# A gated feed-forward stage behind attention: down projection with integer weights and transposed sums

## The reference, cut to what matters

```
q = (qweight nibbles), zp = (z + 1) * s          # s: scale of (group, column), z: zero point
W = q * s[group] - zp[group]
gate = ln(x) @ Wg ;  up = ln(x) @ Wu             # 512 -> 1376
inter = gate * sigmoid(gate) * up
out = (inter @ Wd).astype(float16)               # 1376 -> 512, 11 groups of input rows
x = x + tanh(g_ffn) * out
```

## Time and profile before

| | |
|---|---|
| median of three runs | 739.44 us |
| profiled execution | 740.38 us |
| its span | 738.3 us |
| TensorE busy | 698.6 us (95%) |
| VectorE busy | 582.4 us (79%) |
| ScalarE busy | 431.5 us (58%) |
| GpSimd busy | 226.2 us (31%) |
| granted TensorE clock | 0.999 of full speed |

### The profile page before, as it was taken

How to read it: one execution, slowest core, us unless ns; L and a number is a source line. 1 busy time by engine, 2 the same in 40 slices (tenths; PEclk the granted TensorE clock), 3 DMA queues, 4 the chain that set the end, 5 groups by cost and what they waited for, 6 DMA issues and landing times.

```text
span 738.3 us, 14782 instructions
## 1 busy us (share of the span) xinstructions
PE 698.6 (95%) x5063; PEld 374.4 (51%) x5063; DVE 582.4 (79%) x779; ACT 431.5 (58%) x764; POOL 226.2 (31%) x344
## 2 busy tenths in 40 slices
PE   5879999999999999999999988999999999999997
PEld 4544555455455545554554443445455555555455
DVE  6467788887888887888877488988788778877885
ACT  4866686677677766866775645454444453334443
POOL 5312213222222222132242766583221112222221
PEclk9999999999999999999999999999999999999999
DMA  4112311331233022202202000000000000000101
GB/s 107 32 51 49 89 58 41 93 88 38 59 89 88 8 76 73 60 21 77 73 11 95 8 2 2 1 1 0 1 30 28 1 0 28 28 0 0 43 14 57
DMA packets 29196, 29.90 MB, mean 41 GB/s; under 512 B 18628, under 2 KB 18756, under 8 KB 29036
## 3 DMA queue, kind: packets, MB, share of 16 engines
q1 hardware_dynamic: 26756, 28.80, 14.2%
q10 hardware_dynamic: 2408, 0.70, 0.4%
HBM read 23.49 MB, written 4.23 MB: 38 GB/s over the span
## 4 chain that ended last, share of the span: by engine, by line
PE 66%; POOL 8%; issue 6%; ACT 6%; DMA 6%; DVE 5%; SPq 2%; ACTq 0%; POOLq 0%; DVEq 0%
PE pair L1167 13%; PE small L948 7%; PE pair L905 6%; PE small L919 5%; PE pair L1148 5%; PE pair L1149 5%; PE small L1148 4%; PE small L935 4%; PE small L1149 4%; DMA rn_rows<-rn_parts 3%; POOL rn_sq L407 3%; PE pair L884 3%; ACT eq L616 3%; PE small L985 2%; PE pair L1020 2%
## 5 line engine op out<-in xcount | busy, mean ns | idle before, releaser
L1329 DVE TENSOR_TENSOR eq<-eq,pair 128x1024 f32<-128x1024 f32 x64 | 78.1, 1220 | 52.2 <-PE pair L1002 52.2
L1415 DVE SCALAR_TENSOR_TENSOR acc<-small,scale_T,acc 128x512 f32<-128x512 f32 (+1 forms) x132 | 94.1, 750 | 30.6 <-PE small L1149 30.1
L740 ACT ACTIVATE act_gate<-acc 128x512 f32<-128x512 f32 (+1 forms) x44 | 27.8, 631 | 141.5 <-DVE acc L1415 141.5
L508 POOL TENSOR_TENSOR in_lo<-inter,in_hi 128x512 fp32r<-128x512 f32 (+1 forms) x44 | 56.5, 1283 | 175.2 <-ACT in_hi L747 175.2
L1415 DVE SCALAR_TENSOR_TENSOR acc<-pair,scale_T,acc 128x512 f32<-128x512 f32 (+1 forms) x132 | 94.4, 748 | 16.0 <-PE pair L1149 15.0
L1148 PE MATMUL pair<-ek,w_gu 128*128 (+3 forms) x220 | 85.6, 389 | 8.3 <-DVE acc L1415 6.4
L607 ACT ACTIVATE ek<-pair,kneg 128x512 f32<-128x512 f32 x128 | 86.7, 686 | 10.5 <-DVE kneg L1324 10.4
L1167 PE MATMUL pair<-wd_hi,in_hi 128*128 128x512 f32 (+1 forms) x176 | 87.0, 533 | 0.0
L1167 PE MATMUL pair<-wd_lo,in_hi 128*128 128x512 f32 (+1 forms) x176 | 86.8, 531 | 0.0
L1321 DVE TENSOR_REDUCE qmax<-pair 128x16 f32<-128x1024 f32 x64 | 77.6, 1213 | 8.1 <-PE pair L884 8.1
L1149 PE MATMUL pair<-ekT,w_gu 128*128 (+3 forms) x220 | 83.4, 379 | 0.0
(11 more groups left out here) (159 smaller groups left out, 1329.5 us busy)
## 6 DMA issues: line engine op xcount, KB each, us to landing
xall<-in_x SPq DMA_DIRECT2D x16, 256.0 KB, 2.7
ctx_raw<-in_ctx SPq DMA_DIRECT2D x16, 256.0 KB, 2.9
out_x<-xall SPq DMA_DIRECT2D x16, 256.0 KB, 2.0
zero<-zeros_plus SPq DMA_DIRECT2D x8, 344.0 KB, 5.3
packed<-in_L_ffn_gate_qweight SPq DMA_DIRECT2D x4, 688.0 KB
packed<-in_L_ffn_up_qweight SPq DMA_DIRECT2D x4, 688.0 KB
packed<-in_L_ffn_down_qweight SPq DMA_DIRECT2D x10, 256.0 KB
d_scale<-in_L_ffn_down_scales SPq DMA_DIRECT2D x1, 1408.0 KB, 6.4
```

The lines of the kernel that those rows point to most:

```text
L1329: dve.tensor_tensor(e, e, dve_pair[:, :, :], ALU.mult).then_inc(q_norm, 1)
L1415: dve.scalar_tensor_tensor(out=acc[0:w, it % 3, m, :], in0=gu_bank[job % (2 if first else 4)][0:w, :], scalar=scale_T[0:w, it, 4 * m + g:4 ...
```

## The change

1. **Down projection.** `d_int` becomes fp32r. The product is turned round: the stationary side is a 128-column block nt of the down weights, the moving side the 512 rows of `in_hi` or `in_lo`, the result is transposed (columns on partitions). For blocks 0, 1, 2 the weights are the integers themselves, so there is no low part of the weights: two matmuls each (`high_product`, `low_product`). Their result of each unit (which is also a scale group) has its own scale per partition, so it must be scaled and summed outside PSUM: blocks 0 and 1 by ScalarE (`scaled`, to `y_scaled`) and then GpSimd (`add_sum`), block 2 by VectorE (`add_sum`), in `yT`. Block 3 (`PLAIN`) keeps true weights, three matmuls, and sums in PSUM. A chunk's last sum is written in float16 (`yT16`), TensorE transposes it back (`rows_transposed`, 4 of 128 x 128 for a row tile, in units 3 to 6 of the next chunk), and VectorE adds it to x straight from PSUM.
2. **Gate groups ahead of up groups.** job = 4 m + g. ScalarE takes jobs 0 and 4, VectorE 1, 2, 3, 5, 6, 7. The ring has three banks in all chunks.
3. **Product of gate and up** on GpSimd instead of VectorE (in the last unit still VectorE). `acc`, `in_hi`, `in_lo` have two buffers instead of three.
4. **First chunk.** Only a quarter of the down weights is scaled and split, in two instructions an engine. Inputs 8 to 15 are normalised by ScalarE instead of GpSimd and spread over units 1, 4, 5, 7, 8, 9, 11, 12; the second moments on GpSimd get two instructions more each. Down scales are loaded as 11 more rows of the scales tile and transposed with them, and as 128 columns broadcast to all partitions, both on SP's queue ahead of `step(PAIRS)`.
5. All 44 units are written out; there is no loop.

The core of the diff:

```
+LATE_UNITS = (1, 4, 5, 7, 8, 9, 11, 12)
+PLAIN = slice((NJ - 1) * P, NJ * P)
-        gu_bank = [dve_pair[:, 0, :], dve_pair[:, 1, :], small[0][:, :], small[1][:, :]]
+        gu_bank = [dve_pair[:, 0, :], dve_pair[:, 1, :], small[0][:, :]]
...
 SyncE
-            sp.dma_start(d_scale[:, :, :].rearrange("p g n -> p (g n)"),
-                         matrices[2][1].rearrange("g n -> (g n)").partition_broadcast(P)).then_inc(d_scale_in, 16)
             step(PAIRS - 1, 1, True, True, True, more=False)
             sp.wait_ge(w_int, PAIRS - 2)
             for m in range(2):
                 sp.dma_start(s_rows16[m * GH:(m + 1) * GH, :], matrices[m][1]).then_inc(scales_in, 16)
+            sp.dma_start(s_rows16[2 * GH:2 * GH + IT, 0:N], matrices[2][1]).then_inc(scales_in, 16)
+            sp.dma_start(d_scale[:, :, :], matrices[2][1][:, PLAIN].partition_broadcast(P)).then_inc(d_scale_in, 16)
             step(PAIRS, 0, False, True, True)
...
 GpSimd
+            def activated(n):
+                w = width(n % IT)
+                pool.wait_ge(gs_ready, n + 1)
+                pool.wait_ge(acc_done, 6 * n + 6)
+                if n >= 2:
+                    pool.wait_ge(in_hi_ready, n - 1)
+                    pool.wait_ge(in_lo_ready, n - 1)
+                pool.tensor_tensor(inter[0:w, n % 2, :], act_gate[0:w, :], acc[0:w, n % 2, 1, :],
+                                   ALU.mult).then_inc(inter_ready, 1)
+            def add_sum(n, nt):
+                ...
+                pool.wait_ge(z_act, 2 * n + nt + 1)
+                summed(pool, n - 1, nt)
+                pool.tensor_tensor(yT16[:, nt, :] if it == IT - 1 else total, total, y_scaled[:, nt, :],
+                                   ALU.add).then_inc(z_add, 1)
+            for n in range(UNITS):
+                if n:
+                    activated(n - 1)
+                add_sum(n - 3, 1)
+                if n:
+                    low_part(n - 1)
+                if n == 1:
+                    step(PAIRS + 1, 1, True, False)
+                if n == 2:
+                    second_moments(2)
+                if n == 5:
+                    second_moments(3)
+                add_sum(n - 2, 0)
...
 ScalarE
+            for n in range(UNITS):
+                open_sum(n, 0)
+                if late_input(n - 1):
+                    transposed(late_input(n - 1))
+                ...
+                if n:
+                    high_part(n - 1)
+                else:
+                    transposed(5)
+                    transposed(6)
+                open_sum(n, 1)
+                scaled(n - 2, 0)
+                if n == 0:
+                    transposed(7)
+                silu(n)
+                if n == 0:
+                    act.activation(ident16[:, :], ident[:, :], ACT.Copy).then_inc(ident16_made, 1)
+                    step(PAIRS + 1, PAIRS // 2, 1, False, False, True, drain=True)
+                    plain_high()
+                    ffn_normalised(8)
+                    ffn_normalised(9)
+                scaled(n - 2, 1)
+                if n > IT and n % IT == 1:
+                    plain_sum(n // IT - 1)
+                if late_input(n) and late_input(n) < PAIRS - 2:
+                    ffn_normalised(late_input(n) + 2)
...
 TensorE
+            def high_product(n, nt):
+                ...
+                if n and nt == 2:
+                    pe.wait_ge(z_dve, n)
+                elif n and nt < 2:
+                    pe.wait_ge(z_act, 2 * (n - 1) + nt + 1)
+                if nt == NJ - 1:
+                    pe.matmul(z_bank[nt], wd_hi[0:w, it, :], in_hi[0:w, n % 2, :], start=it == 0, stop=False)
+                    pe.matmul(z_bank[nt], wd_lo[0:w, it, :], in_hi[0:w, n % 2, :], start=False, stop=False)
+                else:
+                    pe.matmul(z_bank[nt], d_int[0:w, it, nt * P:(nt + 1) * P], in_hi[0:w, n % 2, :], start=True, stop=False)
+            for n in range(UNITS):
+                j, it = divmod(n, IT)
+                for job in range(8):
+                    gate_up(n, job)
+                    if n >= 2 and job < NJ:
+                        high_product(n - 2, job)
+                    elif n >= 2:
+                        low_product(n - 2, job - NJ)
+                    if n <= LATE_UNITS[-1]:
+                        rest_of_attention(n, job)
+                    if j and job == 3 and 3 <= it < 3 + TPC:
+                        rows_transposed(j - 1, it - 3)
...
 VectorE
+            for n in range(UNITS):
+                j, it = divmod(n, IT)
+                add_sum(n - 3, 2)
+                for job in range(8):
+                    if job % GH:
+                        add_group(n, job)
+                    if n <= LATE_UNITS[-1] + 1:
+                        rest_of_attention(n, job)
+                if j and 3 <= it < 3 + TPC:
+                    fed_forward(j - 1, it - 3)
+            last_activated()
+            add_sum(UNITS - 3, 2)
+            add_sum(UNITS - 2, 2)
+            last_low_part()
+            for nt in (0, 2, 1):
+                add_sum(UNITS - 1, nt)
+            for t in range(TPC):
                 fed_forward(CHUNKS - 1, t)
```

More of the change, by code:

```diff
@@ L479, in second_moments @@
                 first, count = ln2_parts[part]
-                before, work = 9 * part, ln2_work[:, first:first + count, :]
+                before, work = 11 * part, ln2_work[:, first:first + count, :]
                 pool.wait_ge(bn2_done, first + count)
@@ L494, in ffn_normalised, with plain_scaled @@
                                    ALU.subtract, ALU.mult).then_inc(xn2_ready, 1)
[L496 to L504, removed]
+            def plain_scaled():
+                pool.wait_ge(f_mm, PAIRS)
+                pool.wait_ge(w_int, PAIRS - 2)
+                pool.wait_ge(d_scale_in, 16)
+                for its in (slice(0, IT - 1), slice(IT - 1, IT)):
+                    rows = P if its.start == 0 else width(IT - 1)
+                    pool.tensor_tensor(wd[0:rows, its, :], d_int[0:rows, its, PLAIN].bitcast(F32),
+                                       d_scale[0:rows, its, :], ALU.mult).then_inc(d_scaled, 1)
@@ new lines, in plain_high, with scaled @@
+            def plain_high():
+                for part, its in enumerate((slice(0, IT - 1), slice(IT - 1, IT))):
+                    rows = P if its.start == 0 else width(IT - 1)
+                    act.wait_ge(d_scaled, part + 1)
+                    act.activation(wd_hi[0:rows, its, :], wd[0:rows, its, :], ACT.Copy).then_inc(d_hi, 1)
+            def scaled(n, nt):
+                if n < 0:
+                    return
+                j, it = divmod(n, IT)
+                act.wait_ge(z_mm, NJ * n + nt + 1)
+                if n:
+                    act.wait_ge(z_add, adds_done(n - 1, nt))
+                act.activation(y_scaled[:, nt, :] if it else yT[:, nt, :], z_bank[nt], ACT.Copy,
+                               scale=d_scale_T[:, nt, it:it + 1]).then_inc(z_act, 1)
@@ new lines, in plain_sum, with ffn_normalised @@
+            def plain_sum(j):
+                act.wait_ge(z_mm, NJ * IT * (j + 1))
+                if j:
+                    act.wait_ge(yT_mm, TPC * j)
+                act.activation(yT16[:, NJ - 1, :], z_bank[NJ - 1], ACT.Copy).then_inc(y_plain, 1)
+            def ffn_normalised(k):
+                part = [n for n, (start, _) in enumerate(ln2_parts) if k >= start][-1]
+                act.wait_ge(ln2_step, 11 * (part + 1))
+                act.wait_ge(xT_mm, k - 3)
+                act.activation(xn2[k % 4], xall[:, k, :], ACT.Identity, bias=ln2_work[:, k, 5:6],
+                               scale=ln2_work[:, k, 6:7]).then_inc(xn2_ready, 1)
@@ new lines, in gate_up @@
+                count = 8 * n + job
+                if count >= 3:
+                    n_was, job_was = divmod(count - 3, 8)
+                    if job_was % GH == 0:
+                        pe.wait_ge(s0_done, 2 * n_was + job_was // GH + 1)
+                    else:
+                        pe.wait_ge(acc_done, groups_done(n_was, job_was))
+                lhsT = w_gu[:, m, g, it * P:it * P + w]
+                rows = slice(j * CHUNK, (j + 1) * CHUNK)
+                pe.matmul(gu_bank[count % 3][0:w, :], lhsT, xT_hi[:, g, rows], start=True, stop=False)
```

436 lines of the change are left out of this document (214 added, 222 removed).

## The result

The changed kernel took 734.34 us (median of 5 runs, 733.95 to 735.95) against 741.74 (5 runs, 739.3 to 743.89) of the kernel before beside it: ratio 0.990, 95% interval 0.988 to 0.992. It is faster, as forecast, but by 7.4 us and not by 15.6. The profiled execution took 733.95 (span 732.1), where the sum made for such an execution said 724.8: 9.15 more.

A forecast was written before the change was run, and what follows sets the result against it. TensorE's matmul issue was taken as the bound in three chunks. First chunk 8.3 plus three chunks 9.8, less start 0.4 and tail 2.1, saves 15.6 us: 724.8 profiled, 724 median; own range 718 to 730, 8 in 10 711 to 737.

The forecast's parts named there:

- Matmul count and spacing: TensorE, feed-forward units: 25 instead of 28 matmuls at 0.2275 us each, so 5.69 us a unit instead of 6.37.
- The accumulations: VectorE, each unit: 750 ns alone, 0.72 us apart in a row; seven are 5.04 us of 5.69.
- the 0.14 by which its bank was to be met: Ordinary units: VectorE's sum of block 2 ends before TensorE wants the bank at 1.82 us, met by 0.14.
- the stall that I had forecast: TensorE loses 0.58 us at block 2's bank behind a residual addition, four units a chunk; 2.3 us a chunk.
- Three banks, GpSimd's rate, no stretch: Units: three gate-up banks cost nothing; GpSimd's four instructions take 1.28 us each; VectorE's accumulations beside them stay at 750 ns.
- First chunk: First feed-forward chunk: 75.2 us instead of 83.5, 8.3 saved, bounds 3 and 12; unit 2 begins at 16.0.
- Start of the stage: Before the feed-forward stage: two more ScalarE scale copies lose 0.4 us; the scale loads' DMA 0, at most 3.
- Tail: After the last unit: 12.9 us instead of 10.8, 2.1 lost, bounds 0 and 4.
- Rival (a): Units: GpSimd becomes the bound, about 6.0 us a unit, some 12 us more, 736; chance 0.15.
- (b): VectorE's extra sum never meets TensorE, the 0.58 stalls and most of the first chunk's vanish: 713; chance 0.15.
- (c): Three-bank ring locks with the loop GpSimd product, ScalarE high part, up opening, VectorE job 5: 758; chance 0.09.
- (d): Start: ScalarE's long unit 0 and DMA delay cost 8 us instead of 1: 731; chance 0.11.

The follow-up runs named there:

- e7: e6 with gate and up groups alternating as in e1; 710.69 us, ratio 0.959.
- e10: e7 with the product of gate and up on VectorE again; 708.69 us, ratio 0.954.
- e1: Changed kernel with gate and up groups alternating again and ScalarE opening both sums first; 721.17 us, ratio 0.972.
- e6: Changed kernel, gate groups still first, with block 3's product before block 2's, residual addition behind group 3, and the edits of e4 and e5; 718.91 us, ratio 0.971.
- e7b: e7 with the start of the changed kernel; 713.55 us, ratio 0.961.
- e5: Changed kernel with ScalarE's fourth-block high part and last two normalised tiles moved into the second unit, VectorE's low part to group 7; 733.55 us, ratio 0.990.
- e4: Changed kernel with VectorE's block 2 sum of unit 41 ahead of the last product instead of after it; 732.39 us, ratio 0.987.
- e2: Changed kernel with TensorE's high products of the plain block at job 2 and of block 2 at job 3; 723.38 us, ratio 0.975.

## Why the prediction came out as it did

- **Matmul count and spacing: right.** 25 at 0.2275 are 5.69; e7 and e10 run units of 5.65. Four transposes cost 0.23, where I had set 0.4. The Trainium skill ("TensorE: Matmul & The Clock Gate", Part 4: PE-mode transpose) gives about 275 ns for one. Paid one after another, as I had read it, four would be an estimated 1.1 us and e7's units with them 6.75 instead of 5.88, which the runs exclude. As the duration of one, the figure is near the 222 ns of this trace: here they overlap in a stream of matmuls.
- **The accumulations: the step that failed.** "An accumulation is 750 ns alone, 0.72 apart in a row" was read from the kernel before, where neighbours in the order belong to different sums. Those rows have two in 1.42 us at 0.75 each, which is 0.67 apart and not 0.72, and no two neighbours of one sum. I kept the rate for an order in which each reads the one before. There it is 0.85 to 0.86. The two links ahead of block 2's sum (jobs 5 to 6 and 6 to 7) put it 0.26 later, more than the 0.14 by which its bank was to be met. It was missed in ordinary units by 0.2 (5.86 against e7's 5.65), and units behind a residual addition took 6.74 where 5.69, 0.4 and 0.58 had been laid out: there the total was near (6.67), the parts were not. Over three chunks it is 5.0 us; e1 takes back 9.9 with the order alone, so the interleaved order also does without some of the stall that I had forecast.

Why 0.2, when 0.26 less 0.14 is 0.12: the wait feeds itself. It delays job 4, this delays ScalarE's second opening, and this job 5's accumulation. One ordinary unit shows the ring:

```profile
631.46 0.49 PE L1250 MATMUL pair<-in_hi,d_int 128*128 128x512 f32 x1
...
633.35 0.69 ACT L782 ACTIVATE acc<-pair,scale_T 128x512 f32<-128x512 f32 x1 [0.24 <-PE pair L1227]
...
634.14 0.75 DVE L1529 SCALAR_TENSOR_TENSOR acc<-small,scale_T,acc 128x512 f32<-128x512 f32 x1 [0.37 <-ACT acc L782]
...
635.00 1.60 DVE L1529 SCALAR_TENSOR_TENSOR acc<-pair,scale_T,acc 128x512 f32<-128x512 f32 x2
...
636.52 0.74 DVE L1572 SCALAR_TENSOR_TENSOR yT<-pair,d_scale_T,yT 128x512 f32<-128x512 f32 x1
...
637.31 0.50 PE L1250 MATMUL pair<-in_hi,d_int 128*128 128x512 f32 x1
```

From one high product of block 2 to the next: 1.89 to the opening, 0.79 to job 5's accumulation, 0.86 and 0.85 for the links, 0.67 to the sum, 0.79 to the next product, 5.85 in all. This ring, not TensorE, sets the unit. With the forecast's 0.72 in each of the three places it would be 5.63, below TensorE's own 5.69.

- **Three banks, GpSimd's rate, no stretch: right.** The lines after, from 516 to 716 us, answer to the earlier trace rows: accumulations 749 and GpSimd's 1282 and 1277 ns, though GpSimd works beside VectorE most of the time. The exception is in the tail, where two SBUF inputs still meet GpSimd.

```profile
L1529 DVE SCALAR_TENSOR_TENSOR acc<-pair,scale_T,acc 128x512 f32<-128x512 f32 (+1 forms) x130 | 97.3, 749 | 18.9 <-ACT acc L782 9.6 <-PE small L1227 0.5
L565 POOL TENSOR_TENSOR yT<-yT,y_scaled 128x512 f32<-128x512 f32 (+1 forms) x60 | 76.9, 1282 | 14.2 <-ACT y_scaled L813 13.4
...
L552 POOL TENSOR_TENSOR in_lo<-inter,in_hi 128x512 fp32r<-128x512 f32 (+1 forms) x32 | 40.9, 1277 | 2.2 <-ACT in_hi L797 2.2
```

- **First chunk: right within 1.1 us**. ScalarE opened unit 1 at 11.2 us (forecast 11.7); unit 2 began at 16.7 (16.0, within the bounds). From the one to the other it took 5.5 us instead of 4.3: the sum had no term for TensorE's lower clock there. The granted clock over 440 to 452 us was 0.86 in the changed kernel and 1.00 before.
- **Start of the stage: no loss seen** where 0.4 was set, and one profile can't tell it. The stage of the changed kernel and its variants began later the lower the granted clock was over the first 50 us, where all have the same work: at 432.5 (e6) and 433.2 (e7b) with 1.00, at 434.0 with the 0.97 of the changed kernel's profile, at 435.9 (e5) with 0.90. The kernel before, with 1.00, began at 434.1.
- **Tail: mis-sized.** 12.9 was forecast, 16.7 came, inside none of the bounds (10.8 to 14.8). The working had the last low part done at 3.8 us. VectorE's order puts it behind two sums of block 2, those of units 41 and 42, and the second waits for TensorE:

```profile
720.72 0.75 DVE L1572 SCALAR_TENSOR_TENSOR yT<-pair,d_scale_T,yT 128x512 f32<-128x512 f32 x1 [2.31 <-PE pair L1262]
721.38 1.07 DVE L1547 TENSOR_TENSOR in_lo<-inter,in_hi 96x512 fp32r<-96x512 f32 x1
```

So the low part ended at 7.1 (722.45, counted from 715.4), the last residual addition at 13.2 where 9.7 was forecast, and the output took 3.6 instead of 3.2. e4 takes 1.4 us off in the profile (15.3), of which 1.0 is its order and 0.4 the clock; the rest of the low part's lateness, behind unit 42's sum, is still in it (it ends at 5.8).
- **Rival (a)**, GpSimd as the bound, gave 736, near the time measured, and for the wrong reason: e1 and e6 have the same GpSimd work and run units of 5.67. **(b)**, the sum that never meets TensorE, is what e2 and e7 build; **(c)**'s lock through GpSimd's product did not form, a smaller one through block 2's bank did (the ring above); **(d)** did not occur.

## What to carry to other kernels

An engine's rate "in a row" is a property of the order it was measured in: before moving work, look whether neighbours will read each other's results, and price that link by itself. A wait on the largest line of the list (41.7 us, ScalarE for GpSimd) can be worth nothing, while one of 9.4 us in TensorE's row, with the 22.5 of its weight loads, marked the loss. And offloading work from an engine that isn't full buys nothing: first mend the order, then ask what still needs to move.

## What the runs showed of the hardware

- Behind an accumulation of 128x512 (fp32, PSUM and SBUF in, SBUF out, 0.75 us) an independent one starts on VectorE after 0.67 us, one that waits for its result after 0.85: the link costs 0.18 us.
- TensorE's granted clock was 0.56 over 719 to 722 us behind 2.19 us of idling (three matmuls in 1.40 us) and 1.00 over the same window of e5 behind 2.20 (three in 0.85): like idling did not give like clocks. In the first chunk it was 0.57 from 446 to 450 behind 2.91 us (matmuls of 0.61).
- Over the first 50 us, with the same work in each, it was 0.90 (e5, e7), 0.93 (e1), 0.97 (the changed kernel) or 1.00 (e6, e7b), and the stage began the later the lower it was: 435.9 and 435.6, 435.0, 434.0, 432.5 and 433.2 us.
- Float16 transposes of 128x128 within a run of matmuls took 0.06 us each (four in 0.23), at a recorded duration of 222 ns of one, as the line of all 48 in three chunks of the changed kernel has it:

```profile
L1281 PE MATMUL small<-ident,yT 128*128 128x128 f16 x48 | 4.8, 222 | 0.0
```

- A VectorE product of two SBUF inputs took 1.07 us where it lay beside GpSimd's addition for 0.52 us, and 0.68 in e4, beside it for 0.04; compare. Accumulations with one input in PSUM kept 749 ns.
